# A test of found candidates in two steps, a redo of six passes a tile instead of seven, five score tiles instead of four, and all engine orders dealt anew

## What is computed

```python
scores = jnp.einsum('bhqd,bhkd->bhqk', q, k) / SCALE          # layer 0: softmax over all 1601
top_scores, top_idx = jax.lax.top_k(scores, 32)                # layer 1: the 32 best
w = jax.nn.softmax(top_scores, axis=-1)
...
x = x + jnp.tanh(g_xattn[0]) * _L0_xattn_ref(...)
x = x + jnp.tanh(g_ffn[0]) * _L0_ffn_ref(...)                  # router, top 2 of 8 experts, GELU
x = x + jnp.tanh(g_xattn[1]) * _L1_xattn_ref(...)
x = x + jnp.tanh(g_ffn[1]) * _L1_ffn_ref(...)                  # self-attention plus top 2 of 8 linear experts
```

## Time and profile before

| | |
|---|---|
| median of three runs | 5476.27 us (5466.68 to 5484.45) |
| the profiled execution's own time | 5464.69 us |
| its span, first to last instruction | 5462.9 us |
| mean granted clock of PE | 0.875 of full |
| busy: PE, DVE, ACT | 4452.0, 4287.1, 3963.7 us |
| HBM traffic over the span | 62 GB/s |

### The profile page before, as it was taken

How to read it: one execution, slowest core, us unless ns; L and a number is a source line. 1 busy time by engine, 2 the same in 40 slices (tenths; PEclk the granted TensorE clock), 3 DMA queues, 4 the chain that set the end, 5 groups by cost and what they waited for, 6 DMA issues and landing times. The chain is left out here.

```text
span 5462.9 us, 111091 instructions
## 1 busy us (share of the span) xinstructions
PE 4452.0 (81%) x34502; PEld 1713.4 (31%) x34502; DVE 4287.1 (78%) x22093; ACT 3963.7 (73%) x5192; POOL 1154.4 (21%) x2648
## 2 busy tenths in 40 slices
PE   4777678898787989698798989897897888888765
PEld 1324124242332424233242424233242333324211
DVE  4457987978888887988888787888878888876771
ACT  1346767878586887778688787876887687877673
POOL 2121112222122222212122222211222122121110
PEclk7778889999798999899899999988898898988776
DMA  4232222322122232222223222322222122220100
GB/s 121 70 79 53 58 68 59 81 65 74 49 66 72 59 80 65 67 57 67 71 60 79 63 76 59 78 68 54 75 62 71 51 75 61 52 61 23 35 25 19
DMA packets 472183, 344.99 MB, mean 63 GB/s; under 512 B 155897, under 2 KB 454140, under 8 KB 471550
## 3 DMA queue, kind: packets, MB, share of 16 engines
q1 hardware_dynamic: 471550, 337.54, 24.4%
HBM read 230.12 MB, written 107.13 MB: 62 GB/s over the span
## 5 line engine op out<-in xcount | busy, mean ns | idle before, releaser
L943 DVE MAX8 cand<-s 128x8 f32<-128x67 f32 (+1 forms) x12288 | 1986.2, 222 | 174.0 <-DVEq L1083 122.0
L914 ACT ACTIVATE prob<-wide 128x1024 f32<-128x1024 f32 (+1 forms) x1792 | 1735.0, 1031 | 233.0 <-PE wide L631 102.7
L1029 DVE TENSOR_REDUCE part<-score 128x1 f32<-128x1024 f32 (+1 forms) x1024 | 1003.5, 980 | 303.5 <-PE score L586 261.3
L680 PE MATMUL att<-prob,v 128*9 128x256 f32 (+1 forms) x14336 | 1193.8, 412 | 21.1 <-ACT prob L914 19.7
L895 ACT ACTIVATE s<-wide 128x1024 f32<-128x1024 f32 (+1 forms) x1024 | 821.8, 841 | 390.2 <-DVEq L1083 232.5
L631 PE MATMUL wide<-q,k_att 64*128 64x256 bf16 (+1 forms) x6656 | 700.0, 288 | 260.1 <-ACT s L895 120.8
L904 ACT ACTIVATE below<-wide 128x1024 bf16<-128x1024 f32 (+1 forms) x832 | 819.3, 1027 | 74.6 <-PE wide L631 71.7
L1272 POOL TENSOR_SCALAR flag<-cand,ends 128x24 bf16<-128x24 f32 x512 | 178.9, 349 | 2460.0 <-DVE ends L968 1959.9
L656 PE MATMUL wide<-below,minus_ident 128*128 128x512 bf16 (+1 forms) x1664 | 527.7, 405 | 120.5 <-ACT below L904 104.2
L586 PE MATMUL score<-k_scan,q 64*128 64x512 bf16 (+1 forms) x2048 | 451.5, 365 | 183.2 <-DVE part L1029 159.4
L601 PE MATMUL wide<-k_scan,q 64*128 64x512 bf16 (+1 forms) x2048 | 430.0, 368 | 144.9 <-ACT s L895 79.7
(11 more groups left out here) (161 smaller groups left out, 5124.8 us busy)
## 6 DMA issues: line engine op xcount, KB each, us to landing
k_stack<-split_b SPq DMA_DIRECT2D x576, 128.0 KB, 2.4
k_att<-k_stack SPq DMA_DIRECT2D x768, 96.0 KB, 2.3
k_scan<-k_stack SPq DMA_DIRECT2D x512, 96.0 KB, 2.3
ctxT<-in_ctx_dram SPq DMA_DIRECT2D x32, 800.5 KB, 4.5
k_scan<-k_stack SPq DMA_DIRECT2D x512, 48.0 KB, 1.8
q<-q_stack SPq DMA_DIRECT2D x256, 96.0 KB
q_stack<-split_b SPq DMA_DIRECT2D x192, 64.0 KB, 2.1
self_stack<-split_b SPq DMA_DIRECT2D x192, 64.0 KB, 2.1
```

What stands on the lines that cost most here:

```text
L680: r = tensor.matmul(att[32 * j:32 * j + HD + 1, 0:S], v[0:kc, c, j0 * HG + j, :], m.prob[n % 3][0:kc, j * S:(j + 1) * S], start=(c == 0), ...
L914: scalar.activation(pr[0:kc, :], ps[0:kc, :], ACT.Exp, scale=SCALE).then_inc(sem["wide_done"], 1)
L943: i = vector.max(cand[:, :, c], s[:, KCUT[c]:KCUT[c + 1]])
L1029: vector.tensor_reduce(m.part[:, QT * hh + qt, c:c + 1], score[:, 0:wd], AX.X, ALU.max).then_inc(sem["score_max"], 1)
```

## The change

Four things change.

1. The step `check` is cut in two. `count` takes the largest sum and frees `small`; `check`, later in DVE's list, loads the register, branches and signals `checked`, now one count instead of two.
2. The redo leaves out its first pass over each tile: the 8 best of a tile stand in `ends[:, n, 0, :]` already, since the merge finds these rightly in any case.
3. Five score buffers `m.s` in place of four; the copy of tile n waits for the check of tile n - 5.
4. All five lists of `ORDER` and all `LAG` numbers are dealt anew. The steps are the same, with `count` added.

```diff
+HELD = 5
...
-    z_max=("score_max", 1), n0_all=("n0_ready", 1), check=("checked", 2), least=("least_done", 5),
+    z_max=("score_max", 1), n0_all=("n0_ready", 1), count=("counted", 1), check=("checked", 1), least=("least_done", 5),
...
     dve="""
-        n0_all rank n0_max rank*2 n0_max check rank*2 n0_max rank least rank n0_max rank*2 n0_max rank*2 n0_max rank
+        n0_all rank o_norm.0 n0_max count rank check rank n0_max rank*2 n0_max rank*2 n0_max count rank check rank
...
-        m.s = [sb(f"s{n}", [P, NK]) for n in range(4)]
+        m.s = [sb(f"s{n}", [P, NK]) for n in range(HELD)]
...
-                        if tile >= 4:
-                            q.wait_ge(sem["checked"], after("check", (tile - 4) // 8, (tile - 4) % 8 // QT))
-                        scalar.activation(m.s[tile % 4][:, a0:a0 + wd], ps[:, 0:wd],
+                        if tile >= HELD:
+                            q.wait_ge(sem["checked"], after("check", (tile - HELD) // 8, (tile - HELD) % 8 // QT))
+                        scalar.activation(m.s[tile % HELD][:, a0:a0 + wd], ps[:, 0:wd],
                                           ACT.Copy).then_inc(sem["wide_done"], 1)
...
+                    elif name == "count":
+                        q.wait_ge(sem["small_full"], after("flag", *key))
+                        vector.tensor_reduce(m.many[:, :], small[0:1, 0:QT * (KC + 1)], AX.X,
+                                             ALU.max).then_inc(sem["counted"], 1)
+
                     elif name == "check":
                         g, pair = key
-                        done, tile = before(name, *key), scan_tile(g, QT * pair)
-                        q.wait_ge(sem["small_full"], after("flag", *key))
-                        if done:
-                            q.wait_ge(sem["checked"], done)
-                        vector.tensor_reduce(m.many[:, :], small[0:1, 0:QT * (KC + 1)], AX.X, ALU.max).then_inc(sem["checked"], 1)
-                        q.wait_ge(sem["checked"], done + 1)
+                        tile = scan_tile(g, QT * pair)
+                        q.wait_ge(sem["counted"], after("count", *key))
                         vector.reg_load(many_reg, m.many[0:1, 0:1])
...
-                                best = [ends[:, QT * pair + n, 0, :], m.top_again[:, 0, :], m.top_again[:, 1, :],
-                                        ends[:, QT * pair + n, 1, :]]
-                                for i in range(TOPK // 8):
-                                    if i:
-                                        vector.match_replace(s[:, :], best[i - 1], s[:, :], NEG).then_inc(redo, 1)
-                                        steps += 1
-                                        vector.wait_ge(redo, steps)
+                                s, best = m.s[(tile + n) % HELD], m.ends[g % 2][:, QT * pair + n, :, :]
+                                best = [best[:, 0, :], m.top_again[:, 0, :], m.top_again[:, 1, :], best[:, 1, :]]
+                                for i in range(1, TOPK // 8):
+                                    vector.match_replace(s[:, :], best[i - 1], s[:, :], NEG).then_inc(redo, 1)
+                                    steps += 1
+                                    vector.wait_ge(redo, steps)
```

More of the change, by code:

```diff
@@ L167 @@
+        "route_exp.z": 5, "z_moe_out": 10, "o_copy.0": 3, "ln_copy.v": 3, "route_exp.v": 3, "row_minus.2": 20,
+        "v_gelu": 24, "w_k_out.0": 4, "ln_copy.w": 1, "w_v_out.0": 4, "exp_z": 40, "w_q_out": 1, "att_copy.2": 20,
         "ln_copy.u": 3, "u_q_out": 3, "w_k_out.1": 8},
     dve={
-        "n0_all": 9, "rank": 478, "n0_max": 128, "check": 61, "least": 16, "o_norm.1": 17, "x_add.1": 5,
-        "ln_stats.z": 5, "ln_aggr.z": 5, "ln_scale.z": 5, "route_best.z": 5, "ln_stats.w": 1, "route_pick.z": 5,
@@ L171 @@
-        "z_add": 10, "ln_aggr.w": 1, "o_norm.0": 9, "x_add.0": 3, "z_max": 40, "ln_scale.w": 1, "ln_stats.v": 3,
-        "ln_aggr.v": 3, "ln_scale.v": 3, "route_best.v": 3, "route_pick.v": 3, "v_add": 24, "x_add.v": 3,
-        "o_norm.2": 20, "ln_stats.u": 3, "ln_aggr.u": 3, "ln_scale.u": 3, "x_add.z": 5},
+        "n0_all": 9, "rank": 482, "o_norm.0": 10, "n0_max": 128, "count": 62, "check": 62, "least": 16,
+        "o_norm.1": 17, "x_add.1": 5, "ln_stats.z": 5, "ln_aggr.z": 5, "ln_scale.z": 5, "route_best.z": 5,
@@ L174 @@
+        "route_pick.z": 5, "z_add": 10, "x_add.0": 3, "z_max": 40, "ln_stats.v": 3, "ln_aggr.v": 3, "ln_scale.v": 3,
+        "route_best.v": 3, "route_pick.v": 3, "ln_stats.w": 1, "ln_aggr.w": 1, "v_add": 24, "ln_scale.w": 1,
+        "o_norm.2": 20, "x_add.v": 3, "ln_stats.u": 3, "ln_aggr.u": 3, "ln_scale.u": 3, "x_add.z": 5},
     pool={
-        "shift.0": 9, "mark": 121, "shift.1": 16, "ln_pow.z": 5, "split.z_qk": 10, "ln_pow.w": 1, "ln_pow.v": 3,
-        "shift.2": 20, "split.w_k.0": 4, "split.w_q": 1, "ln_pow.u": 3, "split.u_q": 3, "split.w_k.1": 8},
@@ L177 @@
-    sp={
[3 rows of a table removed]
+        "mark": 122, "shift.0": 9, "shift.1": 16, "ln_pow.z": 5, "split.z_qk": 10, "ln_pow.v": 3, "shift.2": 20,
+        "ln_pow.w": 1, "split.w_k.0": 4, "split.w_q": 1, "ln_pow.u": 3, "split.u_q": 3, "split.w_k.1": 8},
+    sp={
[3 rows of a table added]
         "ctx_in.1": 2, "split_out.w_k.1": 8, "x_out": 5, "x_in": 0},
@@ L250, in streams @@
     of("mark", "mark", [(n,) for n in range(QT * HG * NG)])
-    for name in ("flag", "check"):
+    for name in ("flag", "count", "check"):
         of(name, name, [(g, hh) for g in groups for hh in range(HG)])
@@ L489, in small_drain @@
                 return "z_v_out", key
-            return "check", key
+            return "count", key
         def stored(name, key):
@@ L521, in claim @@
                             q.wait_ge(sem["routed"], before(drain, *of) + 1)
-                        elif drain == "check":
-                            q.wait_ge(sem["checked"], before(drain, *of) + 1)
                         else:
@@ L931, in candidates @@
                 def candidates(tile, part):
-                    s, cand = m.s[tile % 4], m.cand[tile % 3][:, 8:].rearrange("p (k c) -> p k c", c=KC)
+                    s, cand = m.s[tile % HELD], m.cand[tile % 3][:, 8:].rearrange("p (k c) -> p k c", c=KC)
                     cs = range(part * KC // 4, (part + 1) * KC // 4)
```

142 lines of the change are left out of this document (70 added, 72 removed), and 6 rows, old and new, of the table sp.

## The result

The changed kernel takes **5513.18 us** (median of 7 runs, 5502.75 to 5545.35). The kernel before took 5476.27 us in the same comparison (7 runs, 5454.38 to 5484.45). The ratio is **1.0094, 95% interval 1.0073 to 1.0116**: 0.9% slower, where 1.7% faster was forecast. (The two medians alone are 0.7% apart.) The profiled execution has a span of 5527.4 us and a mean granted clock of 0.865; before it was 5462.9 us and 0.875.

What follows compares the result with a forecast made beforehand. DVE and PE were taken to bound the kernel by turns. From the profiled 5464.7 us, 29 (redo) and 65 (check) came off, giving 5371; the median's 11.6 us offset made it 5383 us, range 5290 to 5462.

Steps and rivals of the forecast that it cites:

- The redo, -29 us: In the 8 redos, two passes of 1.83 us fewer each, bare on all engines, come off whole: 29 us less.
- The hole goes: DVE's idle time behind each check, 181 us in all, is mostly covered by the step between count and check.
- 38 us of remainder: Part of the hole behind the checks expected to stay: 0.15 us for each of 256 checks.
- my 143 us: DVE time expected to be gained from the two-step check: 181 - 38 us, with bounds 0 and 181.
- 0.45 of DVE's time becomes time, -65 us: Of the 143 us that DVE gains at the checks, somewhat under half shortens the kernel: 65 us less.
- DVE is full in half of the lap: Ground for the 0.45: DVE is taken as full in about half of each lap, one batch's stretch.
- only the redo gets shorter: Rival: the hole stays or PE is the bound where it goes; 5447 us, 5430 to 5470, chance 0.20.
- Orders anew, 0: The newly dealt lists of all engines hold the same steps and durations; taken as 0 us.
- Five buffers, 0: Fifth score buffer lets ACT run one tile further ahead of the checks: 0 to -49 us, taken as 0.
- Bunched maxima, +153 us: Rival: in DVE's new list, maxima in a row wait bare for PE's score; 5536 us, chance 0.13.
- the 350 us that I had set as its mark: Sign: the wait of `n0_max` for PE's score stays near 261 us; at over 350 the bunching costs.
- The ends: Before 1024 and behind 4514 us: unpriced; a change of over 20 us there would make the forecast wrong.

Runs made afterwards that it cites:

- old_six: The kernel before with the first pass over each tile left out of the redo, nothing else: ratio 0.9954 to the kernel before.
- old_six_five: The kernel before with six passes a tile in the redo and five score buffers, old orders, check in one step: ratio 0.9923 to the kernel before.
- old_split: The kernel before with only the check cut in two steps; old orders, seven passes, four buffers: ratio 1.0006 to the kernel before.
- old_work: The kernel before with one unused MEMSET added on DVE behind each check, 124 us of work in all: ratio 1.0021 to the kernel before.
- half_old: The kernel before with each first-layer maximum taken over half of its columns: ratio 0.9923 to the kernel before.
- new_joined: The changed kernel with only the split taken back, check right behind count in DVE's list: ratio 1.0167 to the kernel before.
- new_q3: The changed kernel with a third q tile in the first layer and all its loads issued one group earlier: ratio 0.9933 to the kernel before.
- old_all: The kernel before with the two-step check, six passes and five score buffers, but the old orders: ratio 0.9939 to the kernel before.
- new_q3_samelag: The changed kernel with a third q tile, the loads left at their place in SP's list: ratio 1.0098 to the kernel before.
- new_q3_joined: new_q3 with the split taken back, check right behind count: ratio 1.0016 to the kernel before.
- old_q3: old_six_five with a third q tile and its loads issued one group earlier: ratio 0.9929 to the kernel before.

## Why the prediction was wrong

Forecast 5383 us, range 5290 to 5462; measured 5513. Step by step:

**The redo, -29 us: right.** old_six measures 25 us. In old_six_five a lap with a redo is 25.0 us longer than one without (before 29.2), in the changed kernel 20.0.

**The hole goes: right, and so is its size.** By the instruction that ends a check it went from 180.8 to 0.8 us, but some 37 us still stand right behind the checks (the row of `cand` alone has 31.2 us under "issue"); I had 38 us of remainder. It is smallest where an `n0_max` or a `z_max` stands in between (2 us over 100 checks); where a rank part stands in between, 48 of 94 checks keep 0.28 us each, 13 us in all. The Trainium skill ("Advanced Engine Details and Errata", Engine Queue Depths) gives VectorE's queue 8 places, by which I had a rank part of 8 instructions covered too; the trace agrees only in part, and the gain came out nearer my 143 us than 181.

**0.45 of DVE's time becomes time, -65 us: wrong.** With the orders that I had reasoned on, up to 137 us of holes removed gave 0 (old_split, at best 0.1%), 124 us of work added cost 11 us (old_work), and 402 us of work removed gave 42 (half_old). My "DVE is full in half of the lap" came from one stretch of 24.8 us. I had counterevidence in hand: 261.3 us of waiting for `score`, and more for `small`, into which a removed hole can pass. The rival "only the redo gets shorter" was the right case for the old orders. With the new ones the split is worth 40 to 45 us, over a quarter of the 156 us of holes that new_joined shows, though DVE waits even more for `score` there (464.8 us, 383.1 in new_q3). So the sum of an engine's waits doesn't decide it either. Why the orders differ in this is not settled; the new ones were only run with either all splits or none.

**Orders anew, 0: wrong, and this decides.** It measured +85 us (the changed kernel beside old_all). I compared DVE's list with care, looked at PE's only through it, and at SP's not at all. new_q3_samelag and new_q3 differ in one number of SP's list and by 1.65% (1.0098 and 0.9933), some 90 us. 60 us are stops of PE on these loads. PE's busy time differs by 23.4 us between the changed kernel and new_q3 for equal work; the two together are 83 us. The question that I left out: for every buffer whose reload waits for its last reader, how many steps now lie between that reader and the next use, and what stands ahead of the reload in the list that issues it?

**Five buffers, 0: slightly short.** 17 us, inside my bound of -49.

**Bunched maxima, +153 us: right in sign, by luck.** The changed kernel is slower, but for another reason. The wait of `n0_max` passed the 350 us that I had set as its mark, and that mark misled: 464.8 us in the changed kernel, 383.1 in new_q3, which is 1.6% faster. Of the rise of 204 us, 122 stay in new_q3, which is as fast as old_all; the other 82 went with the late loads, so there DVE waited for a PE that waited for its q tile. What the 122 cost by themselves is open: without the split something of the new lists costs 0.9% (new_q3_joined beside old_q3). A wait seen from its receiver doesn't say why the sender was late.

**The ends: the warning came true.** I had said that the forecast is wrong if the start changes by over 20 us, and that no row priced it. It changed by 43.6; new_q3 gets 25.9 of them back. What the other 18 us are was not tried, and the laps of new_q3 make up for them (298.7 us without redo, 301.4 before; 322.9 with one, 330.6 before).

## What to carry to other kernels

When the orders of several engines are dealt anew, go through the lists for each buffer: from its last reader, past the load that waits for it, to its next user, and count the steps in the engine's list that must cover the load; do this for the transfers' queue as well as the engines. A further buffer alone does not help if the queue's list brings the load to the same late place. Idle time between two instructions of an engine can be worth nothing or a good part of itself, and neither the engine's share of busy time nor the sum of its waits told which here; add a little work at the same place and time it before counting on the gain. Take the best parts apart: here the old orders with six passes and five buffers (0.9923) and the new ones with early loads (0.9933) are equal, and 1.6 to 1.7% better than the changed kernel.

## What was not expected of the hardware

A stop of PE can cost more than its length. In the changed kernel PE is busy 4470.8 us at a mean granted clock of 0.865; without the stops for `q` it is 4447.4 us at 0.876 (new_q3), for the same matmuls. One stop shows how. Four stretches of the changed kernel, ahead of a wait for `q` (2.70 us in the timeline, until 2251.24), in it, behind it, and then:

```profile
2240.00:2248.50 8.50, 7.46 (x82) 2.27 (x81) 7.35 (x39) 8.28 (x12) 3.75 (x8) 1.00 0.55 138
2248.50:2251.20 2.70, 0.05 (x1) 0.00 (x0) 0.98 (x8) 1.48 (x3) 0.63 (x2) 1.00 0.66 168
2251.90:2256.00 4.10, 4.10 (x30) 0.83 (x28) 3.66 (x17) 2.96 (x3) 0.00 (x0) 0.59 0.02 2
2256.00:2262.00 6.00, 5.42 (x47) 1.62 (x51) 5.66 (x27) 5.75 (x7) 2.02 (x6) 1.00 0.15 29
```

PE was busy 7.46 of 8.50 us at the full 2.4 GHz, stood for 2.70 us, and then had the lower level, 1.2 GHz, for most of 4.10 us in which it was busy without a pause (0.59 in the mean); behind that the full level is back.

A DVE that looks 78% busy took 124 us of new work for 11 us of time, and gave up to 137 us of idle time back for none.
